# Averaging two columns over the partitions: one fp32 product, or one fp32r product of four rounded columns

## What is computed

```python
# first layer; x, y: (32, 128, 1024), weights 128 x 128, 8 heads of 16
q, k = conv1x1(Wq, bq, y), conv1x1(Wk, bk, y)
v = conv1x1(Wv, bv, x)
attn = softmax(einsum('bhdl,bhel->bhde', q, k) / sqrt(E))
out = einsum('bhde,bhel->bhdl', attn, v).reshape(B, E, Lx)
o = conv1x1(Wo, bo, out) + x
mu = mean(o, axis=(1, 2)); var = var(o, axis=(1, 2))
h = (o - mu) * rsqrt(var + 1e-5) * gn_w + gn_b
# second layer: q of h, k and v of y, each with a low-rank (LoRA) part,
# 32 heads of 32 over 8 key heads, softmax, output product, plus h
```

## Time and profile before

| what | value |
|---|---|
| median of 3 runs | 1301.26 us |
| lowest, highest | 1298.92, 1303.53 us |
| span of the profiled execution | 1299.2 us |
| PE busy | 1286.0 us (99%), 6836 instructions |
| PE weight loads busy | 1020.4 us (79%) |
| DVE busy | 916.4 us (71%), 2068 instructions |
| ACT busy | 826.2 us (64%) |
| POOL busy | 150.5 us (12%) |

### The profile page before, as it was taken

One profiled execution on the slowest core, in us unless ns is written; L12 is line 12 of the kernel. 1 busy time (PEld: TensorE's weight loads), 2 busy tenths in 40 slices (PEclk: granted clock), 3 DMA queues, 4 the chain that ended last, 5 costly groups with the idle time before them and its releaser, 6 DMA issues.

```text
span 1299.2 us, 22960 instructions
## 1 busy us (share of the span) xinstructions
PE 1286.0 (99%) x6836; PEld 1020.4 (79%) x6836; DVE 916.4 (71%) x2068; ACT 826.2 (64%) x2900; POOL 150.5 (12%) x117
## 2 busy tenths in 40 slices
PE   8999999999999999999999999999999999999999
PEld 6788888888888888888888888667776776766677
DVE  6677767777657777777777766797676676766665
ACT  6676766666507777777577775766665666655441
POOL 4344443223200000000000005100000000000000
PEclk9999999999999999999999999999999999999999
DMA  9688889889658777878678879989999999988882
GB/s 315 208 272 276 274 266 307 296 297 298 229 190 246 229 226 235 232 232 230 202 226 227 231 217 310 265 238 262 255 259 251 241 256 262 254 223 230 227 227 90
DMA packets 191785, 318.67 MB, mean 245 GB/s; under 512 B 21136, under 2 KB 85904, under 8 KB 190960
## 3 DMA queue, kind: packets, MB, share of 16 engines
q1 hardware_dynamic: 191664, 317.22, 83.8%
HBM read 232.20 MB, written 84.93 MB: 244 GB/s over the span
## 4 chain that ended last, share of the span: by engine, by line
PE 95%; DVE 2%; DMA 1%; SPq 1%; issue 1%; ACT 1%; DVEq 0%; ACTq 0%
PE bank L652 26%; PE bank L702 23%; PE bank L533 13%; PE bank L723 8%; PE bank L756 5%; PE bank L767 5%; PE bank L605 3%; PE bank L518 2%; PE bank L623 2%; DMA lora_raw_q<-in_factors_q 1%; PE bank L638 1%; PE bank L560 1%; PE bank L577 1%; PE bank L507 1%; PE bank L584 1%
## 5 line engine op out<-in xcount | busy, mean ns | idle before, releaser
L986 ACT ACTIVATE bank<-bank,negs 128x128 f32<-128x128 f32 x1024 | 347.4, 340 | 176.9 <-DVE negs L1264 176.6
L652 PE MATMUL bank<-hT,wq 128*128 128x512 f32 x1488 | 390.3, 400 | 0.0
L702 PE MATMUL bank<-wo,op 128*128 128x512 f32 (+1 forms) x1356 | 345.9, 393 | 0.4 <-issue 0.4
L652 PEld LDWEIGHTS bank<-hT,wq 128*128 128x128 f32 x1488 | 264.0, 189 | 46.3
L702 PEld LDWEIGHTS bank<-wo,op 128*128 128x128 f32 x1356 | 249.7, 189 | 52.0 <-issue 1.6
L1259 DVE TENSOR_REDUCE maxes<-bank 128x4 f32<-128x512 f32 x256 | 175.8, 687 | 135.3 <-PE bank L723 135.2
L1003 ACT ACTIVATE probT<-bank 128x512 f32<-128x512 f32 x256 | 151.9, 604 | 111.6 <-PE bank L756 110.0
L986 ACT ACTIVATION_READ_ACCUMULATOR bank<-bank,negs 128x1 f32 x1024 | 209.5, 205 | 0.0
L533 PE MATMUL bank<-wkv_hi,yT 128*128 128x512 f32 x512 | 206.6, 422 | 0.9 <-POOL wkv_lo L1548 0.6
L723 PEld LDWEIGHTS bank<-k_stack,q_stack 96*128 96x128 f32 x1024 | 150.3, 191 | 17.4 <-issue 1.5
L723 PE MATMUL bank<-k_stack,q_stack 96*128 96x128 f32 x1024 | 147.3, 266 | 1.3 <-DMA q_stack<-q_dram 1.3
(11 more groups left out here) (145 smaller groups left out, 1553.3 us busy)
## 6 DMA issues: line engine op xcount, KB each, us to landing
q_stack<-q_dram SPq DMA_DIRECT2D x256, 256.0 KB, 4.1
q_dram<-q_part SPq DMA_DIRECT2D x64, 512.0 KB, 4.1
q_stack<-q_dram SPq DMA_DIRECT2D x256, 128.0 KB, 4.5
yT_in<-in_ctx_turned SPq DMA_DIRECT2D x32, 512.0 KB, 4.5
y_in<-in_ctx SPq DMA_DIRECT2D x32, 512.0 KB, 7.2
x_in<-in_x SPq DMA_DIRECT2D x32, 512.0 KB, 5.6
h_dram<-h_out SPq DMA_DIRECT2D x32, 512.0 KB, 8.0
h_in<-h_dram SPq DMA_DIRECT2D x32, 512.0 KB, 3.7
```

What stands on the lines that cost most here:

```text
L652: m = pe.matmul(bank(u % 2).rearrange("p (a n) -> p a n", a=2), wq[:, block, part, c, :], hT[(group + 1) % 2][:, :, of, c, :], start=c == ...
L702: mm = pe.matmul(place[:, columns], op[m][:, of, c, :], wo[m][w][:, c, columns], start=c == 0 and of == 0 and w == 0, stop=c == GROUP - 1 ...
L986: act.activation(part, part, ACT.Exp, bias=negs[:, n % RING, j:j + 1], scale=SCORE1, accum_out=sums[:, score_column(k), g, j:j + 1]).then_ ...
```

## The change

`ones_avg` becomes a tile of fp32r (rounded fp32, the type of the kernel's large products). VectorE splits the two columns into a rounded part and the rest, `stat_parts` (128 x 2 x 2); one fp32r product averages the four columns; and VectorE adds the two halves of the result into `stat_sums`, from which `deviation` and `norm_factors` now read. The small bank is free once this sum is made. `deviation(b-1)` now stands ahead of `norm_factors(b-2)`. `var_product` stays an fp32 product.

```diff
--- before.py
+++ after.py
@@ -99,13 +99,15 @@
                 table[m] = sb(f"{name}_{m}", [P, HID + COLS[m]], dt)
 
         factor_tiles(lora, "lora", F32R, "kv", "o")
-        ones_avg = sb("ones_avg", [P, P])
+        ones_avg = sb("ones_avg", [P, P], F32R)
         first = sb("first", [P, 6 * P + 5])
         w0T, wv0, bqk = first[:, 0:3 * P], first[:, 3 * P:4 * P], first[:, 4 * P:6 * P].rearrange("p (a n) -> p a n", a=2)
         score_bias = sb("score_bias", [P, P])
         bq_col, bv_col, bo_col, gnw_col, gnb_col = (first[:, 6 * P + i:6 * P + i + 1] for i in range(5))
         bq_scaled = sb("bq_scaled", [P, 1])
         minus_half = sb("minus_half", [P, 1])
+        stat_parts = sb("stat_parts", [P, 2, 2], F32R)
+        stat_sums = sb("stat_sums", [P, 2])
         y_sum = sb("y_sum", [P, 2])
         gram_mixed = sb("gram_mixed", [P, P])
         gram = sb("gram", [P, P])
@@ -210,7 +212,7 @@
             "wo_out0", "wo_out1", "wo_out2",
             "yT_hi", "yT_lo", "ysum", "gram_mm", "gram_m", "gram_h", "gram_turn", "gram", "t1_mm", "t1", "sbq",
             "s_mm", "s_sb", "s_max", "s_neg", "s_exp", "s_rec", "att", "n1_mm", "n1", "mix_mm",
-            "mix", "mix_hi", "mix_lo", "xbias", "x_hi", "x_lo", "mx_mm", "bn", "agg", "st",
+            "mix", "mix_hi", "mix_lo", "xbias", "x_hi", "x_lo", "mx_mm", "bn", "agg", "st", "st_hi", "st_lo", "st_sum",
             "st1_mm", "dev", "nm", "st2", "st2_mm", "ve", "pow", "gsc", "gbi", "h", "kv_mm",
             "kv", "kv_keys", "kT_mm", "kT_hi", "kT", "h_out0", "h_out1", "kv_out0", "kv_out1", "stack_ones",
             "h_in0", "h_in1", "hT_mm", "hT_hi", "hT_lo", "q_mm", "q_hi", "q_lo", "q_out0", "q_out1",
@@ -273,10 +275,10 @@
             small_uses += [(("gram", b), "gram", b + 1), (("t1", b), "t1", b + 1), (("s", b), "s_sb", b + 1),
                            (("n1", b), "n1", b + 1), (("mix", b), "xbias", b + 1)]
             if b:
-                small_uses += [(("st", b - 1), "nm", b), (("prep", unit_of(b)), "prep_merged", unit_of(b) + 1)]
+                small_uses += [(("st", b - 1), "st_sum", b), (("prep", unit_of(b)), "prep_merged", unit_of(b) + 1)]
             if b - 1 >= LATE_STATS:
                 small_uses.append((("var", b - 1), "ve", b))
-        small_uses += [(("kT", B - 1), "kT", B), (("st", B - 1), "nm", B), (("var", B - 1), "ve", B),
+        small_uses += [(("kT", B - 1), "kT", B), (("st", B - 1), "st_sum", B), (("var", B - 1), "ve", B),
                        (("prep", N_UNITS - 1), "prep_merged", N_UNITS)]
         small = {key: bank(6 + i % 2) for i, (key, _, _) in enumerate(small_uses)}
         small_freed = {key: small_uses[i - 2][1:] for i, (key, _, _) in enumerate(small_uses) if i >= 2}
@@ -544,14 +546,14 @@
 
                 ps = small_bank("st", b)
                 pe.wait_ge(S["const"], CONST["stats"])
-                pe.wait_ge(S["st"], b + 1)
-                pe.wait_ge(S["st2"], b)
-                pe.matmul(ps[:, 0:2], ones_avg[:], both_st, start=True, stop=True).then_inc(S["st1_mm"], 1)
+                pe.wait_ge(S["st_lo"], b + 1)
+                pe.matmul(ps[:, 0:4], ones_avg[:], stat_parts[:].rearrange("p a n -> p (a n)"), start=True,
+                          stop=True).then_inc(S["st1_mm"], 1)
 
             def var_product(b):
                 ps = small_bank("var", b)
                 pe.wait_ge(S["st2"], b + 1)
-                pe.matmul(ps[:, 0:1], ones_avg[:], st2, start=True, stop=True).then_inc(S["st2_mm"], 1)
+                pe.matmul(ps[:, 0:1], f32(ones_avg[:]), st2, start=True, stop=True).then_inc(S["st2_mm"], 1)
 
             def t1_product(b):
                 ps = small_bank("t1", b)
@@ -1152,10 +1154,23 @@
                 dve.bn_aggr(mv, bn[:].rearrange("p a b -> p (a b)")).then_inc(S["agg"], 1)
                 dve.wait_ge(S["agg"], b + 1)
                 dve.tensor_scalar(st, mv[:, 0:1], xbias[b % 2], None, ALU.add).then_inc(S["st"], 1)
+                dve.wait_ge(S["st"], b + 1)
+                dve.wait_ge(S["st2"], b)
+                if b:
+                    dve.wait_ge(S["st1_mm"], b)
+                dve.tensor_scalar(stat_parts[:, 0, :], both_st, 1.0, None, ALU.mult).then_inc(S["st_hi"], 1)
+                dve.wait_ge(S["st_hi"], b + 1)
+                dve.tensor_tensor(stat_parts[:, 1, :], both_st, f32(stat_parts[:, 0, :]), ALU.subtract).then_inc(
+                    S["st_lo"], 1)
 
             def deviation(b):
-                mean = small["st", b][:, 0:1]
+                mean = stat_sums[:, 0:1]
                 dve.wait_ge(S["st1_mm"], b + 1)
+                if b:
+                    dve.wait_ge(S["nm"], b)
+                dve.tensor_reduce(stat_sums[:], small["st", b][:, 0:4].rearrange("p (a n) -> p n a", a=2), AX_X,
+                                  ALU.add).then_inc(S["st_sum"], 1)
+                dve.wait_ge(S["st_sum"], b + 1)
                 dve.tensor_tensor(dev, st, mean, ALU.subtract).then_inc(S["dev"], 1)
                 dve.tensor_tensor(nm[b % 2], xbias[b % 2], mean, ALU.subtract).then_inc(S["nm"], 1)
                 dve.wait_ge(S["dev"], b + 1)
@@ -1164,8 +1179,8 @@
             def norm_factors(b):
 
                 if b < LATE_STATS:
-                    dve.wait_ge(S["st1_mm"], b + 2)
-                    var = small["st", b + 1][:, 1:2]
+                    dve.wait_ge(S["st_sum"], b + 2)
+                    var = stat_sums[:, 1:2]
                 else:
                     dve.wait_ge(S["st2_mm"], b - LATE_STATS + 1)
                     var = small["var", b][:, 0:1]
@@ -1451,9 +1466,9 @@
                     split_hT(0)
                 add_mix(b)
                 rest_yT(b + 1, 1)
+                deviation(b - 1)
                 if 0 <= b - 2 < LATE_STATS:
                     norm_factors(b - 2)
-                deviation(b - 1)
                 if last:
                     split_hT(1)
                 rest_mix(b)
@@ -1539,7 +1554,7 @@
             pool.affine_select(out=mask, in_=mask, compare_op=ALU.is_ge, fill=OFF_BLOCK, base=D0 - 1,
                                pattern=[[D0, H0], [0, D0]], channel_multiplier=-1).then_inc(S["const"], 1)
             pool.memset(minus_half[:], -0.5).then_inc(S["const"], 1)
-            pool.memset(ones_avg[:], 1.0 / P).then_inc(S["const"], 1)
+            pool.memset(f32(ones_avg[:]), 1.0 / P).then_inc(S["const"], 1)
             pool.memset(norm[:], 0.0).then_inc(S["const"], 1)
 
             def prep_rest(n):
```

## The result

The changed kernel takes 1314.34 us (median of 4 runs, 1313.45 to 1315.22); the kernel before takes 1300.09 (median of 4 on the same chip, 1298.73 to 1303.53). The ratio is 1.0102, with a 95% interval from 1.0084 to 1.0119: 1.0% slower. The profiled execution took 1313.93 us, its span is 1312.1 us against 1299.2.

What follows compares the result with a forecast made beforehand. TensorE, 95% of the chain of waits, was taken as the bound. 29 loops x 0.45 = 13.1, + 0.4 + 0.9 = 14.4 us on the 1299.2 span gave 1313.6; with 2.1 to the median, 1315.5 us predicted, range 1303 to 1322.

Steps and rivals of the forecast that it cites:

- No slack at the averaging product: TensorE's wait for `st` in steady batches: next to no slack, the 0.23 us equalling the first loop's; 0.11 at most.
- the release that I took for `st_lo`: Averaging product's wait: release taken as behind `st`, the load starting 0.23 us after its end.
- The saved pass of 0.11: Averaging product on TensorE: fp32r takes one pass, not two, saving 0.11 us for each of 32, 3.6 at most.
- The head: VectorE ahead of the averaging product: its operand ends 0.47 us later (0.37 to 0.64); TensorE 0.36 late, less the pass.
- The prep product: TensorE's wait through `xbias`: 0.5 us later against 0.17 of slack at most, so reached 0.33 to 0.4 late.
- VectorE's path: VectorE through a batch: 0.58 us more behind the product, 1.06 late in all, 0.58 idle; grows by 0.48, period by 0.45.
- They can't collide: Loops other than first and last: GpSimd's `lower_x` comes behind `power`, and `power` behind `dev`, so no collision.
- First loop: `st_lo` held by GpSimd's `lower_x` until 33.7, but prep product waited anyway: 0.4 us in the end (0 to 1).
- Last loop: `dev` and `nm` read SBUF twice beside `lower_x`, making `st2` late and `var_product` wait: 0.9 us (0 to 1.9).
- Hidden and the pass won: Rival: VectorE's additions fit into slack at TensorE's waits, leaving 3.4 us less, 1297.9 us; chance 0.11.
- Costs more than its loads show: Rival: fp32 averaging product costs more, say a type switch, VectorE hidden: 7.1 us less, 1294; chance 0.05.
- the fourth rival: Above 0.65 us a batch, or waits drop the clock again, 1 to 2 us each time: 1322 to 1330, chance 0.08.

Runs made afterwards that it cites:

- x5: Kernel before plus only the part behind the product (averages copied to SBUF, deviation reading them there, norm_factors ahead of it): 1305.34 us for 1301.20, ratio 1.0032.
- x4: Kernel before plus only the two VectorE split instructions ahead of the product, which stays fp32 and waits for the second: 1310.41 us for 1301.20, ratio 1.0077.
- x1: Kernel before with the fp32 averaging product issued twice, the first copy into spare columns: 1307.45 us for 1301.20, ratio 1.0046.
- x3: Changed kernel with the four-column sum taken out of deviation and norm_factors put straight behind it, ahead of deviation: 1309.23 us for 1301.77, ratio 1.0057.
- x2: Kernel before with the two columns written rounded as fp32r, one fp32r averaging product, no second part: 1298.51 us for 1301.20, ratio 0.9982.
- x6: x3 with the split moved behind add_mix and the averaging product behind the prep product: 1304.67 us for 1301.77, ratio 1.0021.

## Why the prediction was right, step by step

The time (1315.5 forecast, 1314.3 measured), the sign and the sum (14.4 us forecast; 14.25 between the medians) hold. Single terms were off in both directions. Part of the agreement is luck: between the spans the change costs 12.9 us, of which the like loops make 11.2 where 13.1 were forecast, and the kernel before had a median of 1300.09 this time, 1.2 under the one that I had added to. The sum itself has a slip (1313.6 + 2.1 is 1315.7, not 1315.5), and its lower bound of 0.2 us a loop is worked out nowhere; the text gives 0.34 for VectorE's path.

**No slack at the averaging product: right; the release that I took for `st_lo`: wrong.** In the kernel before, the load comes 0.23 to 0.27 us behind the end of `st` in all loops from 1 to 30, never less than the 0.23 of the first loop, where TensorE stood waiting. x5 has two steady loops in which it waited too, and there it is 0.23 again (load at 54.56, `st` from 54.12 to 54.33). So the slack was 0 to 0.04. But behind `st_lo` the load starts 0.12 us after the end, not 0.23. That is why 0.40 us more ahead of the product make the loop only 0.28 longer (x4).

**The saved pass of 0.11: right** (x1: 0.22 to 0.235 for two; 206.66 - 206.55 = 0.11 in the trace). The Trainium skill (FP8 and Floating Point Precision, TensorE Precision Notes) counts four passes for true fp32. The trace has two pairs of a weight load and a matmul for each product, and the time agrees with two: at 0.11 us for each of four, x1 would have cost an estimated 14 us.

**The head, 0.47 forecast, too large.** `st_hi` starts 0.24 after `st` although it waits for three semaphores (I took 0.35); that is no more than the 0.25 from L1152 to L1154 with one. With 0.21 for `st_lo` and 0.16 of its own, it ends 0.61 after `st`'s start instead of 0.68. Less the pass, TensorE loses 0.17 to 0.18 a loop (x3), where I forecast 0.36.

**The prep product: wrong slack.** I compared `xbias` with the start of the load and found 0.17. But that load ran 0.22 us ahead of its matmul; a load that is held has its matmul 0.11 behind it, so there were 0.28 us from the end of `xbias` to the latest start that holds nothing up. `xbias` came 0.40 later, and the load needs 0.05 behind it. What is left is 0.17, and not 0.33 to 0.4.

**VectorE's path: right.** Head 0.40 (0.48 forecast) and tail 0.57 (0.58 forecast) against idle time of 0.58 to 0.63: 0.34 to 0.39, measured 0.34 in the median loop, and forecast as 0.45 with 0.34 as the lower bound. That it is the larger of the two paths was the decisive choice, and x3 and x5 confirm it: without the tail's growth the loop goes to 0.17, without the head's it goes to 0.04. The cover behind `lower_x`, costed at nothing, held as well: `mixed_x` loads `x_lo` 1.4 to 1.8 us after it is ready.

**"They can't collide": wrong.** I had excluded a collision with GpSimd in loops 2 to 30. In two of them GpSimd also prepares the factors of the output weights, and its last operation then reached VectorE's L1215, a 128x128 operation from SBUF to SBUF:

```profile
86.08 1.29 POOL L1563 TENSOR_TENSOR wq<-w_raw,wq 128x512 fp32r<-128x512 f32 x1
...
86.61 0.84 DVE L1215 TENSOR_SCALAR att<-att,att_stat 128x128 f32<-128x128 f32 x1
```

0.84 us instead of 0.29, and the like once before (0.91 at 54.05). The loops 2, 3, 5 and 6 around them are together 1.0 us longer than the others. It is the later tail that brings them together: x5 has the same two collisions, x4 and the kernel before have none. Four more loops (4, 8, 11 and 21) were 0.2 to 0.3 us longer by a single late start on VectorE, in x3 likewise in 4 and 8, less in 11 and not in 21; their cause stays open. The longer loops are why the mean grew by 0.40 and the median by 0.34, so that it is partly luck that the mean is near my 0.45.

**First loop: right place, half the mechanism.** 0.4 forecast, 0.45 measured (45.33 for 44.88). Held was already `st_hi`, with a single input in SBUF, and not only `st_lo`.

**Last loop: right.** `dev` took 1.79 us instead of 0.15, `var_product` waited 1.35 us; 0.28 + 0.94 = 1.2 us, 0.9 forecast.

```profile
356.56 2.36 POOL L1609 TENSOR_TENSOR x_lo<-x_in,x_hi 128x1024 fp32r<-128x1024 f32 x1 [6.79 <-ACT x_hi L914]
...
357.15 1.79 DVE L1174 TENSOR_TENSOR norm<-norm,stat_sums 128x1 f32<-128x1 f32 x1
...
359.37 0.30 PEld L556 LDWEIGHTS bank<-norm,ones_avg 128*128 128x128 f32 x2 [1.35 <-issue]
```

**The rivals.** "Hidden and the pass won" needed 0.5 us of slack at both waits; x4 shows that there was not. "Costs more than its loads show" fell with x1 and x2. The clock fell behind the first loop in the changed kernel as it had before: 0.67 from 34.6 to 38.3 us and 0.61 from there to 39.5, for 0.54 and 1.00 before. Either way that is an estimated 1.7 us (0.46 x 3.7; 0.33 x 3.7 + 0.39 x 1.2). It fell nowhere else, and its mean is 0.999 in both profiled executions. That waits can make it fall once more, the part of the fourth rival, came true in x6 and not here.

## What to carry to other kernels

Where two engines hand a chain to and fro, follow each engine's path through a loop by itself and take the larger: here one grew by 0.17 us and the other by 0.34, and mending the larger gave back only the difference. A wait without idle time need not have slack: compare its distance with that of a place where the engine surely stood waiting, for the same pair of instructions, and use the starts of matmuls, since loads run ahead. Trading a TensorE pass of 0.11 us for dependent VectorE instructions of 0.2 us each paid at neither of the two places tried here, since the product waited for them at both; to write the operand in the wanted type in the first place added no instruction and won.

## What was not expected of the hardware

- GpSimd's 128x1024 operation held back not only VectorE's operations with two inputs in SBUF (2.31 instead of 0.68 us before), but also one with a single input and two columns (2.06 instead of 0.17) and one with two inputs and one column (1.79 instead of 0.15). One with a single input of 128 columns was held as well, by GpSimd's 128x512 operation (0.84 instead of 0.29). Operations of one column with one tensor input in SBUF ran beside `lower_x` unhindered (L1193 at 209.27 took 0.21 us), and so did those with an input in PSUM (L1135 at 210.38 took 0.28).
- The release from VectorE to TensorE differs: 0.22 to 0.23 us behind `st`, 0.12 behind `st_lo`, 0.05 to 0.06 behind `xbias`, each the same in every loop from 1 to 30 in which TensorE stood waiting.
- A small product of one pass alone among large ones costs 0.11 us (L543), and 0.19 if its weight load comes only 0.04 us ahead of its matmul (L550 in x6); as one more of a group of small ones, 0.11 (x1, the changed kernel).
- One gap of 1.97 us between weight loads in the last loop was followed by about 6 us with a mean granted clock of 0.71 (x6), an estimated 1.7 us beside the wait itself.
